# Splitting weights at other times, and a TensorE that works before its tokens come

## The chip, the cores and the metric

The kernel runs on one core of a Trainium2 chip. The metric is the device time of one launch in microseconds (us). Weights, tokens and scratch tensors lie in the chip's memory; all sums are fp32 sums of products of split fp32 numbers, as told below.

## The reference

```python
xn = layernorm(x)                          # x is (8, 1024, 512), no scale or shift
local  = softmax(q @ k.T / sqrt(128)) @ v  # q, k, v = xn @ local_qkv_w, head 128
sparse = the same with sparse_qkv_w, scores below the 102nd largest of their row left out
xp  = xn @ memory_proj_w                   # memory head, 64 memories
mem = concat(xp, softmax(xp @ bank.T) @ bank) @ mem_out_w + mem_out_b
pred = gelu((xn @ pred_in_w + b) @ pred1_w + b) @ pred2_w + b
s = concat(local, sparse, mem, pred) @ warboss_w + warboss_b     # "mixing" weights, 512 x 512
g = silu(relu(xn @ w1 + b1) @ w2 + b2)     # FFN, width 2048 = 16 chunks of 128
out = x + s * g
```

## The kernel before

Every product of two fp32 matrices is made of three products on TensorE (`product`, L70 to L74): each operand is split into a high part (a copy rounded to the type fp32r) and a low part (value minus high part), and high x high, high x low and low x high are summed. A split costs one or two evictions on ScalarE (ACT): the value and its high part; and one subtraction, on VectorE (DVE, helper at L646) or on GpSimd (POOL, helper at L487).

Stage 1 goes through the tokens in 16 halves n = 0 to 15 of 512 tokens. For each half TensorE runs 18 jobs in the order of a list (`JOBS`, and `FIRST_JOBS` for n = 0), each into one of six PSUM banks: mp and pi (12 products of 512 columns each: memory projection, input of the prediction), ql, qs, kl, ks (queries and keys, 12 each), ms (memory scores), p1a, p1b and p2 (prediction), wt (transposed memory weights), tr0 to tr3 (the next half's normalised tokens transposed, 16 transposes of 128x128 in all), mo (memory output), v01 and v23 (values, 24 products of 256 columns each). ScalarE evicts the jobs in the same order. VectorE makes in each half, in this order: the low parts of mp and pi (`act_lo`), the memory softmax, `gelu_hi` and `gelu_lo` (p2 waits for them), the low part of wt (mo waits for it), the low parts of the four transposed token blocks, and then the layer norm of half n+2 (`layer_norm`, L655 to L686). GpSimd makes the low parts of queries, keys, values, mo, p2 and of one FFN chunk per half (`ffn`, behind kl). SyncE issues all DMAs, in one order with its waits: the next tokens, the stored transposed tokens, keys (`store_kv(0)`), the FFN chunk, the tiles of queries and head outputs (`tile_scratch`), the next raw FFN chunk, values.

Half 0 is special. Tokens of half 0 are loaded in four tiles, normalised, and transposed after the whole normalisation (L869), block by block of columns. ScalarE copies each transposed block twice (`tokens`, L519 to L522), a raw copy and the high part, and VectorE subtracts the two. All projection weights are split here, and so are the four 128-row blocks of the mixing weights: ScalarE makes `ww_hi` behind ql (L619), VectorE makes `ww_lo` (`low_mixing`, L720) in two pairs, before `gelu_hi` and before wt's low part. Layer norm 1 is spread over half 0, layer norm 2 over half 1 (`parts`), whose tokens are loaded late (`load_half` behind `store_kv(0)` for n = 1).

In half 14 and 15 the first steps of stage 2 are mixed in: the sparse scores of tile 0 and the search for their 102nd largest value, 13 rounds on VectorE (`first_search`, MAX8 and MATCH_REPLACE8). Two rounds stand in half 15 between the memory maximum and the memory weights (L806 to L809).

Stage 2 has 64 slots of one 128-token tile each; slot m (from 1) has four FFN chunks (f1: 12 products into `hid`, f2: 12 into `acc`), the scores, transposes (L1618) and head outputs. The first FFN weights that stage 2 reads are the ones that stage 1 stored last: `first_ffn` (L414) loads them when the store of the 16th chunk has landed. In slot 1 the order on TensorE is sparse scores, f1 of chunk 0, transposes, f1 of chunk 1, full scores, f2 of chunk 0, f1 of chunk 2, transposes of the full probabilities. VectorE's search in slot 1 takes the row maximum of the full scores in round 2 (L1456) and the reciprocal of their sum in round 3 (L1462).

Of the kernel before, what the change touches and what calls it, by code (L numbers as in the profile page):

```python
# [42 lines left out]
NEWTON = 3  # L43

# [32 lines left out]
def build(nc, x, w, out):  # L77
# [4 lines left out]
    with ExitStack() as outer:  # L82
# [7 lines left out]
        ww_hi, ww_lo = sb("ww_hi", [P, KT, D], F32R), sb("ww_lo", [P, KT, D], F32R)  # L90
# [7 lines left out]
        with nc.sbuf_tensor("ffn", [P, 2, 2, D], F32R) as ffn:  # L98
            pass
        shared = Shared(  # L100
            ident=ident, ww_hi=ww_hi, ww_lo=ww_lo, b2=b2, half_bias=half_bias, small=small, ranks=ranks,
# [49 lines left out]
class Shared:  # L151
# [3 lines left out]
    ww_lo: object  # L155
    b2: object
# [69 lines left out]
def stage1(nc, outer, x, w, xnT_d, kv_d, tile_d, ffn_d, shared):  # L226
# [8 lines left out]
    SM_LOADS, BIAS_LOADS = 4, 5  # L235
    CONSTS = 3

    with ExitStack() as ctx:
# [30 lines left out]
        ww = xnT_raw[:, 1, :, HI, :]  # L269
# [36 lines left out]
        ww_split = sem("ww_split")  # L306
        ln_step = sem("ln_step")
        xn_ready = sem("xn_ready")
        job_done = sem("job_done")
# [29 lines left out]
        def sync(sp):  # L339
# [30 lines left out]
            sp.dma_start(ww[:, :, :], w["warboss_w"].rearrange("(k p) n -> p k n", p=P)).then_inc(ww_in, 16)  # L370
# [46 lines left out]
            def steps(b):  # L417
                for hh in range(2):
# [9 lines left out]
                    if n < LAST - 1 and n != 1:  # L428
                        load_half()
# [17 lines left out]
                    if n == LAST - 1:  # L447
                        first_local()
                    sp.wait_ge(kv_l, 4 * n + 2)
                    store_kv(0)  # L450
                    if n == 1:
                        load_half()

                    sp.wait_ge(ffn_l, n + 1)
                    sp.dma_start(ffn_d[bass.ds(n, 1), :, :, :, :].rearrange("a p i s n -> p (a i s n)"),
                                 ffn[:, :, :, :].bitcast(F32).rearrange("p i s n -> p (i s n)")).then_inc(ffn_st, 16)
# [6 lines left out]

                    sp.wait_ge(ffn_st, 16 * n + 16)
                    if n < LAST:
                        load_ffn(n + 1)
                    else:
                        first_ffn()
# [8 lines left out]
        def gpsimd(pool):  # L477
# [11 lines left out]
            def steps(b):  # L489
                for hh in range(2):  # L490
# [3 lines left out]
                    for name in (name for name in jobs(n) if name in slots):  # L494
# [18 lines left out]
        def scalar(act):  # L513
# [21 lines left out]
            def steps(b):  # L535
                for hh in range(2):
                    n = 2 * b + hh
                    for name in jobs(n):
# [55 lines left out]
                        else:  # L594
# [6 lines left out]
                            if first(n):  # L601
                                act.wait_ge(ww_split, k + 1)
# [41 lines left out]
        def vector(dve):  # L644
# [127 lines left out]
            def steps(b):  # L772
                for hh in range(2):
# [1016 lines left out]
```

## Time and profile before

| | us |
|---|---|
| median of 3 runs | 2559.91 (2559.63 to 2560.24) |
| the profiled execution, its own time | 2559.92 |
| span of its first to last instruction | 2558.1 |
| TensorE busy | 2519.6 (98%) |
| VectorE busy | 2316.3 (91%) |
| ScalarE busy | 1357.9 (53%) |
| GpSimd busy | 1094.0 (43%) |

The span is told in us from its first instruction. In the rows further down PE is TensorE, PEld its weight loads, SPq the DMA queue that SyncE fills. A row of the timeline has start, duration, engine, line, operation, what is written and what is read, and how often; in brackets stands how long the engine was idle before, and for whom. PEclk is the granted clock of TensorE as a share of 2.4 GHz.

### The profile page before, as it was taken

To read this page: it belongs to the slowest core of one execution; us is meant where nothing else is said; L and a number is where in the kernel's file an instruction comes from. 1 tells how busy PE (TensorE), PEld (TensorE's weight loads), DVE (VectorE), ACT (ScalarE), POOL (GpSimd) and SP (SyncE) were. 2 spreads that over 40 slices of the span, in tenths; PEclk is the share of its full clock that TensorE was granted. 3 is DMA by queue.
4 is the path that set the end of the run, shared out by engine and by line. 5 is a ranking of instruction groups with operands and counts; after the bars stand their busy time and mean duration, and the time that the engine had idled before them with its cause. 6 is when DMAs were issued, how large, how long until landed. Compare 5 with 4: busy or idle time off the path is not lost.

```text
span 2558.1 us, 36958 instructions
## 1 busy us (share of the span) xinstructions
PE 2519.6 (98%) x12884; PEld 2144.0 (84%) x12884; DVE 2316.3 (91%) x5184; ACT 1357.9 (53%) x2304; POOL 1094.0 (43%) x847
## 2 busy tenths in 40 slices
PE   7999999999999999999999999999999999999999
PEld 5788888778888888888888888888888888888887
DVE  6666666889999999999999999999999999999996
ACT  5677777744444444444444444444444444444443
POOL 2444554433444444444444444444444444444443
PEclk9999999999999999999999999999999999999999
DMA  7788788874665466556654665466546654665443
GB/s 235 269 306 320 283 308 337 317 271 157 210 219 198 165 209 221 198 165 208 222 198 165 211 218 199 165 212 213 200 165 212 217 197 165 213 215 197 165 157 124
DMA packets 164568, 551.79 MB, mean 216 GB/s; under 512 B 17888, under 2 KB 30880, under 8 KB 156064
## 3 DMA queue, kind: packets, MB, share of 16 engines
q1 hardware_dynamic: 164384, 549.43, 61.2%
q8 instruction: 104, 1.70, 0.3%
q14 instruction: 80, 0.66, 0.1%
HBM read 415.15 MB, written 134.22 MB: 215 GB/s over the span
## 4 chain that ended last, share of the span: by engine, by line
PE 95%; DVE 2%; DMA 1%; ACT 0%; POOL 0%; SPq 0%; issue 0%; ACTq 0%
PE acc L72 9%; PE hid L74 9%; PE hid L72 9%; PE acc L74 9%; PE acc L73 9%; PE hid L73 9%; PE o L74 5%; PE o L73 5%; PE o L72 5%; PE ps L72 5%; PE ps L74 5%; PE ps L73 5%; PE scores L1618 4%; PE scores L74 2%; PE scores L73 2%; PE scores L72 2%
## 5 line engine op out<-in xcount | busy, mean ns | idle before, releaser
L1360 POOL TENSOR_TENSOR h_lo<-h,h_hi 128x512 fp32r<-128x512 f32 x254 | 333.8, 1314 | 811.9 <-ACT h_hi L1257 811.9
L1488 DVE MAX8 ranks<-early 128x8 f32<-128x512 f32 x819 | 564.3, 689 | 13.0
L1508 DVE MATCH_REPLACE8 early<-ranks,early 128x512 f32<-128x512 f32 x756 | 510.8, 676 | 0.0
L1256 ACT ACTIVATE h<-hid,small 128x512 f32<-128x512 f32 x256 | 176.3, 689 | 500.8 <-PE hid L74 500.8
L72 PE MATMUL acc<-w,h_hi 128*128 128x512 f32 x1016 | 408.2, 402 | 0.0
L72 PE MATMUL hid<-xnT,w 128*128 128x512 f32 x1024 | 399.3, 390 | 7.5 <-DMA w<-ffn_scratch 7.5
L74 PE MATMUL hid<-xnT,w 128*128 128x512 f32 x1024 | 399.6, 390 | 0.0
L73 PE MATMUL hid<-xnT,w 128*128 128x512 f32 x1024 | 398.8, 389 | 0.0
L74 PE MATMUL acc<-w,h_lo 128*128 128x512 f32 x1016 | 396.6, 390 | 0.0
L73 PE MATMUL acc<-w,h_hi 128*128 128x512 f32 x1016 | 396.3, 390 | 0.0
L1360 POOL TENSOR_TENSOR pT_s<-pT,pT_s 128x512 fp32r<-128x512 f32 x256 | 326.8, 1299 | 40.9 <-ACT pT_s L1269 40.9
L1492 DVE MAX8 ranks<-early 128x8 f32<-128x512 f32 x441 | 298.0, 676 | 0.0
L1511 DVE MATCH_REPLACE8 early<-ranks,early 128x512 f32<-128x512 f32 x378 | 255.3, 675 | 0.0
L72 PEld LDWEIGHTS hid<-xnT,w 128*128 128x128 f32 x1024 | 192.6, 188 | 48.0 <-DMA w<-ffn_scratch 7.7
L74 PEld LDWEIGHTS hid<-xnT,w 128*128 128x128 f32 x1024 | 192.5, 188 | 40.1
L73 PEld LDWEIGHTS hid<-xnT,w 128*128 128x128 f32 x1024 | 192.6, 188 | 39.9
L74 PEld LDWEIGHTS acc<-w,h_lo 128*128 128x128 f32 x1016 | 190.7, 188 | 41.7
L73 PEld LDWEIGHTS acc<-w,h_hi 128*128 128x128 f32 x1016 | 191.6, 189 | 33.7
L72 PEld LDWEIGHTS acc<-w,h_hi 128*128 128x128 f32 x1016 | 191.2, 188 | 33.6
L487 POOL TENSOR_TENSOR tiles_out<-tiles_out 128x512 fp32r<-128x512 f32 x64 | 104.6, 1635 | 260.4 <-ACT tiles_out L579 235.9
L1257 ACT ACTIVATE h_hi<-hid,small 128x512 fp32r<-128x512 f32 x254 | 173.1, 682 | 0.0
L1269 ACT ACTIVATE pT_s<-scores 128x512 fp32r<-128x512 f32 x256 | 158.1, 618 | 0.0
(224 smaller groups left out, 5496.3 us busy)
## 6 DMA issues: line engine op xcount, KB each, us to landing
w<-ffn_scratch SPq DMA_DIRECT2D x512, 512.0 KB, 4.0
xnT_scratch<-xnT SPq DMA_DIRECT2D x16, 2048.0 KB, 13.5
kv_scratch<-kv_out SPq DMA_DIRECT2D x32, 1024.0 KB, 7.1
tile_scratch<-tiles_out SPq DMA_DIRECT2D x16, 2048.0 KB, 8.7
tl<-tile_scratch SPq DMA_DIRECT2D x64, 512.0 KB, 4.0
xnT<-xnT_scratch SPq DMA_DIRECT2D x60, 512.0 KB, 6.8
ffn_scratch<-ffn SPq DMA_DIRECT2D x16, 1024.0 KB, 6.6
values<-kv_scratch SPq DMA_DIRECT2D x16, 1024.0 KB, 6.5
```

What stands on the lines that cost most here:

```text
L72: nc.tensor.matmul(out, w_hi, x_hi, start=first, stop=False)
L73: nc.tensor.matmul(out, w_hi, x_lo, start=False, stop=False)
L74: return nc.tensor.matmul(out, w_lo, x_hi, start=False, stop=last)
L487: pool.tensor_tensor(value, value.bitcast(F32), hi.bitcast(F32), ALU.subtract).then_inc(ready, 1)
L1256: nc.scalar.activation(h32[:, c % 2, :], hid[:, :], ACT.Relu, bias=bias)
L1257: nc.scalar.activation(h_of(C, c)[0], hid[:, :], ACT.Relu, bias=bias).then_inc(h_h, 1)
L1269: nc.scalar.activation(pT_s[:, j * HTILES:(j + 1) * HTILES, HI, t, :], scores[:, c].rearrange("p (t n) -> p t n", n=P), ACT.Copy)\
L1360: return nc.gpsimd.tensor_tensor(out_, value, hi_.bitcast(F32), ALU.subtract).then_inc(ready, 1)
L1488: l_step = count(nc.vector.max(top_l[:, own], larger[:, :]))
L1492: s_step = count(nc.vector.max(top_s[:, own_s], smaller[:, :]))
L1508: l_step = count(nc.vector.match_replace(larger[:, :], top_l[:, own], larger[:, :], LOWEST))
L1511: s_step = count(nc.vector.match_replace(smaller[:, :], top_s[:, own_s], smaller[:, :], LOWEST))
```

## The change

1. TensorE transposes the identity 72 times into `scores` before tokens come. The first tokens are then transposed tile by tile, each tile as soon as it is normalised (`tile_ready`).
2. `tokens` evicts only the high part; VectorE takes the raw value of the low part from PSUM. The last quarter of the projection weights is split behind the four token blocks.
3. The mixing weights are loaded into the room of `ww_lo` and split one block each in halves 2 to 5: `ww_hi` behind v23's eviction on ScalarE, `ww_lo` behind the layer norm on VectorE. The waits of tr0 to tr3 in half 0 for this split go. The zero rows of `bm_lo` are written at the very start.
4. Layer norm 2 goes to the end of half 0, its tokens are loaded without the special place, and half 1 has no spread parts.
5. The FFN chunk is split behind ks in half 0 and behind qs later (before: behind kl), and GpSimd no longer waits for wt in halves 14 and 15. From half 1 on it is stored before the keys, and the next raw chunk is loaded (in half 15: `first_ffn`) before the tile store is issued.
6. One search round less in half 15 before the memory weights.
7. Stage 2's first two `load_w2` and their wait for the tile stores move behind `load_w1(2)` in slot 1.

```diff
+WARM = 72
-        ww_hi, ww_lo = sb("ww_hi", [P, KT, D], F32R), sb("ww_lo", [P, KT, D], F32R)
+        ww_hi = sb("ww_hi", [P, KT, D], F32R)
+        with nc.sbuf_tensor("ww_raw", [P, KT, D], F32) as ww_raw:
+            pass
+        ww_lo = sb("ww_lo", [P, KT, D], F32R)
...
+    MIXING_AT, MIXING_BEHIND = (2, 3, 4, 5), "v23"
+    FFN_AT = {True: "ks", False: "qs"}
...
-                    if n < LAST - 1 and n != 1:
+                    if n < LAST - 1:
                         load_half()
...
+                    if not first(n):
+                        store_ffn()
                     sp.wait_ge(kv_l, 4 * n + 2)
                     store_kv(0)
-                    if n == 1:
-                        load_half()
-                    (wait for ffn_l, store of the FFN chunk)
+                    if first(n):
+                        store_ffn()
+                    sp.wait_ge(ffn_st, 16 * n + 16)
+                    if n < LAST:
+                        load_ffn(n + 1)
+                    else:
+                        first_ffn()
                     sp.wait_ge(tiles_l, 4 * n + 4)
                     (store of the tiles)
-                    sp.wait_ge(ffn_st, 16 * n + 16)
-                    (load_ffn(n + 1) or first_ffn())
...
-                        if name == "kl":
-                            if n >= LAST - 1:
-                                pool.wait_ge(lo_ready, lo(n, "wt"))
+                        if name == FFN_AT[first(n)]:
                             pool.wait_ge(ffn_h, n + 1)
                             left(ffn[:, :, LOW, :], ffn[:, :, HI, :], ffn_l)
...
             def tokens(k):
                 act.wait_ge(job_done, k + 1)
-                nc.scalar.activation(xnT_raw[:, 0, k, LOW, :], ps[:, k, :], ACT.Copy)
                 nc.scalar.activation(xnT[:, 0, k, HI, :], ps[:, k, :], ACT.Copy).then_inc(bank_read, 1)
...
-            tokens(0)
+            for k in range(KT):
+                tokens(k)
             weights(KT - 1)
-            for k in range(1, KT):
-                tokens(k)
...
-                            if first(n):
-                                act.wait_ge(ww_split, k + 1)
...
-                        if (n, name) == (0, "ql"):
+                        if name == MIXING_BEHIND and n in MIXING_AT:
+                            k = MIXING_AT.index(n)
                             act.wait_ge(ww_in, 16)
-                            for k in range(KT):
-                                nc.scalar.activation(ww_hi[:, k, :], ww[:, k, :], ACT.Copy).then_inc(w_h, 1)
+                            nc.scalar.activation(ww_hi[:, k, :], shared.ww_raw[:, k, :], ACT.Copy).then_inc(ww_h, 1)
...
+            dve.wait_ge(consts, CONSTS)
+            nc.vector.tensor_tensor(bm_lo[MEM:P, :], ident[MEM:P, :], ident[MEM:P, :], ALU.subtract)
             layer_norm(0)
-            parts = {0: layer_norm_parts(1), 1: layer_norm_parts(2)}
+            parts = {0: layer_norm_parts(1)}
...
-                subtract(xnT[:, 0, k, LOW, :], xnT_raw[:, 0, k, LOW, :], xnT[:, 0, k, HI, :])\
+                subtract(xnT[:, 0, k, LOW, :], ps[:, k, :], xnT[:, 0, k, HI, :])\
...
                     if n == LAST:
                         next(rounds)
-                        next(rounds)
...
-                        low_mixing((0, 1))
...
-                    if first(n):
-                        low_mixing((2, 3))
...
-                    if 0 < n < LAST - 1:
+                    if n < LAST - 1:
                         layer_norm(n + 2)
+                    if n in MIXING_AT:
+                        k = MIXING_AT.index(n)
+                        dve.wait_ge(ww_h, k + 1)
+                        subtract(ww_lo[:, k, :], shared.ww_raw[:, k, :], ww_hi[:, k, :])
...
             pe.wait_ge(consts, CONSTS)
-            pe.wait_ge(xn_ready, 1)
-            for k in range(KT):
-                transposes(k, k).then_inc(job_done, 1)
+            for _ in range(WARM):
+                nc.tensor.transpose(scores[:, 0:P], ident[:, :], ident[:, :])
+            for t in range(HTILES):
+                (wait for tile_ready t + 1, for the last tile xn_ready)
+                for k in range(KT):
+                    last = first_transposes(t, k)
+                    if t == HTILES - 1:
+                        last.then_inc(job_done, 1)
...
-            sp.wait_ge(tiles_st, 16 * HALVES)
-            load_w2(1, 1)
-            load_w2(2, 2)
...
                 load_w1(C + 2, c + 2)
+                if m == 1:
+                    sp.wait_ge(tiles_st, 16 * HALVES)
+                    load_w2(1, 1)
+                    load_w2(2, 2)
                 load_w2(C + 3, c + 3)
```

## Rows read from the trace of the kernel before

**Rows 1.** The waits of TensorE, summed: us in total, times, longest.

```profile
PE hid L72 <- DMA w<-ffn_scratch: 7.5, 1, 7.5
PE ps L72 <- DVE gelu_lo L646: 7.0, 2, 5.7
```

**Rows 2.** Windows: span, its length, busy time of PE, PEld, DVE, ACT, POOL, PEclk, DMA.

```profile
46.70:56.00 9.30, 9.30 (x50) 8.20 (x51) 5.14 (x8) 5.88 (x11) 2.58 (x2) 0.78 0.68 282
...
540.00:2558.00 2018.00, 2012.52 (x10086) 1705.10 (x10084) 1947.04 (x4370) 976.16 (x1571) 849.84 (x687) 1.00 0.57 193
```

**Rows 3.** Timeline, the first 20 us.

```profile
12.87 3.65 PE L869 MATMUL ps<-ident,early 128*128 128x128 f32 x16 [12.87 <-DVE early L684]
13.15 0.84 ACT L517 ACTIVATE wp_hi<-tiles_out 128x768 fp32r<-128x768 f32 x1 [0.51 <-DMA tiles_out<-in_L_attn_sparse_qkv_w]
...
13.99 0.60 ACT L521 ACTIVATE xnT_raw<-ps 128x512 f32<-128x512 f32 x1
...
14.49 0.59 ACT L522 ACTIVATE xnT<-ps 128x512 fp32r<-128x512 f32 x1
...
16.70 0.40 PE L73 MATMUL ps<-xnT,wp_hi 128*128 128x512 f32 x1
...
20.15 0.40 PE L74 MATMUL ps<-xnT,wp_lo 128*128 128x512 f32 x1
```

**Rows 4.** Timeline of VectorE, 36 to 48 us.

```profile
38.19 4.44 DVE L646 TENSOR_TENSOR ww_lo<-xnT_raw,ww_hi 128x512 fp32r<-128x512 f32 x2
42.55 1.75 DVE L833 CAST gelu_hi<-gelu 128x1024 fp32r<-128x1024 f32 x1
44.33 2.16 DVE L646 TENSOR_TENSOR gelu_lo<-gelu,gelu_hi 128x1024 fp32r<-128x1024 f32 x1
```

**Rows 5.** Timeline of TensorE: p2 of half 0, mp of halves 1, 2 and 3, ms.

```profile
46.64 0.77 PE L72 MATMUL ps<-gelu_hi,sm_hi 128*128 128x512 f32 x1 [5.68 <-DVE gelu_lo L646]
...
55.37 0.40 PE L72 MATMUL ps<-xnT,wp_hi 128*128 128x512 f32 x1
...
86.31 0.40 PE L72 MATMUL ps<-xnT,wp_hi 128*128 128x512 f32 x1
...
98.17 0.30 PE L924 MATMUL ps<-bkT_s,act_hi 128*128 128x128 f32 x1 [3.51 <-DVE act_lo L646]
...
120.88 0.40 PE L72 MATMUL ps<-xnT,wp_hi 128*128 128x512 f32 x1
```

**Rows 6.** The chain of waits, full halves: start, us, what.

```profile
136.95 0.44 PE ps L938 x4
...
141.52 1.75 PE ps L869 x16
...
166.09 0.44 PE ps L938 x4
```

**Rows 7.** Timeline, layer norm 2 and the tile store of half 1.

```profile
85.89 0.36 SPq L459 DMA_DIRECT2D tile_scratch<-tiles_out  x1
90.20 2.47 DVE L666 BATCH_NORM_STATS2 small<-early 128x6 f32<-128x512 f32 x4 [5.49 <-DMA early<-in_L_attn_x]
97.34 1.28 DVE L646 TENSOR_TENSOR act_lo<-act,act_hi 128x512 fp32r<-128x512 f32 x2
97.72 0.60 ACT L578 ACTIVATE tiles_out<-ps 128x512 f32<-128x512 f32 x1 [4.48 <-DMA tile_scratch<-tiles_out]
```

**Rows 8.** Timeline, from stage 1 to stage 2.

```profile
499.69 0.47 SPq L455 DMA_DIRECT2D ffn_scratch<-ffn  x1
505.89 1.62 SPq L414 DMA_DIRECT2D w<-ffn_scratch  x2
...
513.35 0.68 DVE L1492 MAX8 ranks<-early 128x8 f32<-128x512 f32 x1
...
521.12 1.22 DVE L1456 TENSOR_REDUCE ranks<-scores 128x1 f32<-128x1024 f32 x1 [7.10 <-PE scores L74]
...
526.36 1.09 PE L1618 MATMUL scores<-ident,early 128*128 128x128 f32 x8
```

More of the change, by code:

```diff
@@ L100, in build @@
         shared = Shared(
-            ident=ident, ww_hi=ww_hi, ww_lo=ww_lo, b2=b2, half_bias=half_bias, small=small, ranks=ranks,
+            ident=ident, ww_hi=ww_hi, ww_lo=ww_lo, ww_raw=ww_raw, b2=b2, half_bias=half_bias, small=small, ranks=ranks,
             xnT=xnT, xnT_raw=xnT_raw, ks=ks, kl=kl, tl0=tl0, tl1=tl1, w10=w10,
@@ L155 @@
     ww_lo: object
+    ww_raw: object
     b2: object
@@ L305, in stage1 @@
         w_first = sem("w_first")
-        ww_split = sem("ww_split")
+        ww_h = sem("ww_h")
         ln_step = sem("ln_step")
         xn_ready = sem("xn_ready")
+        tile_ready = sem("tile_ready")
         job_done = sem("job_done")
@@ L448, in steps, with store_ffn @@
                         first_local()
+                    def store_ffn():
+                        sp.wait_ge(ffn_l, n + 1)
+                        sp.dma_start(ffn_d[bass.ds(n, 1), :, :, :, :].rearrange("a p i s n -> p (a i s n)"),
+                                     ffn[:, :, :, :].bitcast(F32).rearrange("p i s n -> p (i s n)")).then_inc(ffn_st, 16)
+                    if not first(n):
+                        store_ffn()
                     sp.wait_ge(kv_l, 4 * n + 2)
                     store_kv(0)
[L451 to L456 removed]
+                    if first(n):
[5 more added lines that the diff above has]
+                        first_ffn()
                     sp.wait_ge(tiles_l, 4 * n + 4)
@@ L462, in steps @@
                         .then_inc(tiles_st, 16)
-                    sp.wait_ge(ffn_st, 16 * n + 16)
[L465 to L468, printed above, removed]
                     sp.wait_ge(kv_l, 4 * n + 4)
@@ L634, in steps @@
                                 .then_inc(shared.pl_ready, 1)
-                        if name == "kl":
+                        if name == FFN_AT[first(n)]:
                             act.wait_ge(ffn_in, 32 * n + 32)
@@ L685, in layer_norm_parts @@
                                                    rstd[:, t:t + 1], ALU.subtract, ALU.mult)
+                    if first(n) and t < HTILES - 1:
+                        last.then_inc(tile_ready, 1)
                 last.then_inc(xn_ready, 1)
@@ L710, in vector @@
             low_weights(QS, 1)
-            def low_mixing(rows):
-                for k in rows:
-                    dve.wait_ge(w_h, 2 + KT + k)
-                    subtract(ww_lo[:, k, :], ww[:, k, :], ww_hi[:, k, :]).then_inc(ww_split, 1)
             def small_weights():
@@ L823, in steps @@
                         dve.wait_ge(bm_out, 1)
-                        subtract(bm_lo[0:MEM, :], bm[0:MEM, :], bm_hi[0:MEM, :])
-                        nc.vector.tensor_tensor(bm_lo[MEM:P, :], bm[MEM:P, :], bm[MEM:P, :], ALU.subtract)\
-                            .then_inc(bm_split, 1)
-                        low_mixing((0, 1))
+                        subtract(bm_lo[0:MEM, :], bm[0:MEM, :], bm_hi[0:MEM, :]).then_inc(bm_split, 1)
                     if n == LAST:
@@ L873, in tensor, with first_transposes @@
             pe.wait_ge(consts, CONSTS)
-            pe.wait_ge(xn_ready, 1)
-            for k in range(KT):
-                transposes(k, k).then_inc(job_done, 1)
+            for _ in range(WARM):
+                nc.tensor.transpose(scores[:, 0:P], ident[:, :], ident[:, :])
+            def first_transposes(t, k):
+                return nc.tensor.transpose(ps[:, k, t * P:(t + 1) * P], xn[:, t, k * P:(k + 1) * P], ident[:, :])
+            for t in range(HTILES):
+                if t < HTILES - 1:
+                    pe.wait_ge(tile_ready, t + 1)
+                else:
+                    pe.wait_ge(xn_ready, 1)
+                for k in range(KT):
+                    last = first_transposes(t, k)
+                    if t == HTILES - 1:
+                        last.then_inc(job_done, 1)
             def bank_projection():
```

3 lines of the change are left out of this document (1 added, 2 removed).

## The prediction

> **What bounds the kernel now.** I read the shares of busy time first: TensorE is busy for 2519.6 of 2558.1 us, so only the 38.5 us in which it idles, and the stretches in which it runs at its lower clock, are to be had without taking work off it. Then TensorE's waits: 7.5 us for a first-layer FFN weight and 7.0 us for `gelu_lo` [rows 1], and 3.5 us for `act_lo` in half 2 [rows 5]; the 12.9 us before the first transpose are the start itself. Then windows around them. After a long wait TensorE also runs slowly: from 46.7 to 56 the granted clock is 0.78 of full, which is 4.1 us at the level of 1.2 GHz instead of 2.4, or 2.0 us lost on top of the wait [rows 2]. From half 3 on the halves follow each other in 29.14 us (136.95 to 166.09) [rows 6] without a wait. In stage 2 TensorE is busy for 2012.5 of 2018 us, and VectorE for 1947.0 of them [rows 2]: both are nearly full there. So what is late on TensorE up to slot 1 moves the end, as long as VectorE comes along.
>
> The sum is made against the profiled execution, 2559.92 us (span 2558.1, 1.8 us around it). It lies 0.01 us from the median of the runs, so both serve.
>
> **Start (edits 1 and 2).** Now the 16 transposes start at 12.87, when all four tiles are normalised, and take 3.65 us, or 0.23 each; in a full half 16 take 1.75 us, or 0.11 each [rows 3, 6]. The durations say that they run at the lower level (the granted clock has no entry for it there). At 16.70 a product takes the 0.40 us that it also takes at 20.15: the level rose within 3.8 us of the first transpose, with little but transposes before it [rows 3]. So the 72 identity transposes from about 1.8 us on should take 3.8 us for 17 at 0.23 and 6.0 us for 55 at 0.11, and be done at 11.6. Tiles come at about 11.3, 11.8, 12.3 and 12.7 and need 0.44 us each: all blocks are transposed at about 13.3, where it was 16.5.
>
> The next limit is ScalarE. It is in the third weight split until 13.99, released by a DMA [rows 3], which the change leaves. Then four high parts, 0.5 us apart as at 13.99 and 14.49 [rows 3], give blocks at 14.6, 15.1, 15.6 and 16.1. VectorE subtracts in 0.64 us each (two take 1.28, [rows 7]): done at 15.2, 15.9, 16.5 and 17.2. Its source in PSUM has no row with this width; between 0.5 and 1.2 us I take 0.64, the row of the same operation and width. The last three products of mp then run from 17.3 to 18.0; now mp ends at 20.15 plus 0.23, 20.4. Gain 2.4. The last weight split follows at 16.1 to 16.9, before VectorE wants it at 17.2. The zeroing of `bm_lo` at the start lies in front of the first tile's arrival: nothing. If TensorE's 2 us of idleness between 13.3 and 15.3 brings the lower level back, 1.5 to 2 us of the gain go.
>
> The Trainium skill speaks against this step: its page "TensorE: Matmul & The Clock Gate", section "Part 4: PE-mode transpose", says that the full clock does not engage for the transpose mode, since it does not count as TensorE being busy. The rise at 16.70 speaks against the rule here. It has a rival of its own below.
>
> **Half 0 (edits 3 and 5).** VectorE's queue is the limit here. The chain from mp's low part to layer norm 1 moves by 2.4 us as a whole. Behind it go two `ww_lo` of 4.44 us and the zero rows; `gelu_hi` 1.75 and `gelu_lo` 2.16 end at 46.5 [rows 4]. Now `gelu_hi` can start at about 34.5 and `gelu_lo` ends at 36.4 to 38.4, by whether GpSimd's work beside it still slows it to these durations. TensorE would be at p2 at 46.64 minus 5.68 minus 2.4, 38.6 [rows 5]: no wait, and no slow stretch. Next comes mo, for wt's low part, about 0.5 us late, since ScalarE's evictions of v01 and wt set it. p2 to v23 takes 7.2 us: mp of half 1 starts at 45.9 instead of 55.37 [rows 5]. Gain to here 9.4 (7.0 of it in this step). Mixing blocks in halves 2 to 5 cost VectorE 0.64 us each before the low part of mp, and ScalarE one 0.6 us copy. That low part is wanted for ms, 8.2 us after mp's start (94.5 against 86.31 [rows 5]); layer norm and low parts take 7.1 and 0.64, and in a full half the norm starts well before mp. They cost nothing; if this cover were gone, 0.64 each, 2.6 together.
>
> **Layer norm 2 and half 1 (edit 4).** In half 0 the norm now stands between tr3 and half 1's first low part. Its length is 97.34 minus 90.20, 7.1 us [rows 7]. FIRST_JOBS puts tr3 last but one, so tr3's low part ends at about 47.2, with `half_bias` 47.6, the norm 54.8, the low part 55.4. ms could start at 45.9 plus 8.2, 54.1: a new wait of 1.4 us. Behind it lies the tile store: load_ffn and the landing of the FFN store go before it, so it is issued at about 48.5. The store of half 1 took from 85.89 to 97.72 until it let ScalarE on [rows 7], so ql's eviction may come at 57 to 60 where it is wanted at 54.4, with the memory softmax behind it on ScalarE from 58: 0 to 2 us more. I take 2.0 for half 1 in all (0.6 to 3.5). Half 1 lasts 30.94 now (86.31 minus 55.37) and 29.14 plus 2.0 then: 0.2 lost.
>
> **Half 2.** It lasts 34.57 now (120.88 minus 86.31) [rows 5], since its tokens come late and the norm ends at 97.3; the wait is 3.51 and the slow stretch behind it costs the rest. With tokens and norm a half earlier it is a full half: 29.14, gain 5.4. Mp of half 3 then starts at 106.3: 14.6 earlier.
>
> **Halves 3 to 13.** Storing the FFN chunk before the keys issues 1 MB some 3 us earlier, and puts 0.5 MB of raw chunk ahead of the tiles. ScalarE's ql eviction is behind the tile store. No wait of TensorE follows by my reckoning: 0 a half, bounded by 0 and 2 (half a load's 4 us).
>
> **Stage 2's entry (edits 5 to 7).** Now the FFN store is issued at 499.69, lands at 505.89, and the load issued then is there at 515.26, 7.5 us after TensorE wanted it [rows 1, 8]. Behind qs instead of behind kl and wt, GpSimd would be done with the chunk at about 494.5; with no key store before it, it is issued 5 us earlier, lands at about 499.5, and the load, now ahead of the 2 MB of tiles, is in by 505: before TensorE wants it. What is late next is VectorE. It is at the end of its second MAX8 of round 2 at 514.03, then idles 7.10 for the full scores, takes the maximum at 521.12, and TensorE transposes the probabilities at 526.36, 5.24 later, without a wait [rows 8]. Without the load's wait the scores are there at 512 to 513, so VectorE goes on at 514.03, and the transposes come at 519.27. Gain 7.1, VectorE's idle time, and not the 7.5 plus a slow stretch that TensorE has. The moved search round changes nothing in VectorE's sum; it lets the memory weights come 2.5 us earlier but leaves VectorE idle for up to 1.6 before `gelu_hi`, against 1 to 1.7 less slowing by GpSimd. Bounds 5.5 and 8.7. `load_w2(1)` now waits for f1 of chunk 0 and the tile store, issued at about 511, wanted at 520: hidden.
>
> **Sum.** 14.6 plus 7.1 is 21.7: 2559.92 minus 21.7 is 2538.2 us.
>
> **Rivals.**
> A, forecast: 2538.2, own range 2533 to 2542; chance 0.72.
> B, the identity transposes leave the clock low. 72 at 0.23 last till 18.4, the 16 real ones 3.7 us more, till 22.1; mp follows at the low level and ends at about 25 to 26.5 instead of 18. That is 7 to 8.5 lost: 2545 to 2547. For it: nothing in the rows, but they show no transposes of a constant alone. The Trainium skill's rule named above would make it so. Chance 0.10.
> C, the end of the wait in half 0 only makes room for the next: GpSimd and ScalarE, which run beside VectorE, hold wt's low part and the tile store of half 0 so that 3 to 5 us of the 14.6 stay: 2541 to 2544. For it: the 4.48 us of ScalarE behind a tile store [rows 7]. Chance 0.12.
> D, the other side: the raw FFN chunk ahead of the tiles delays each tile store so far that ScalarE's ql eviction, and with it the memory softmax, comes too late for wt in every half. Twelve halves lose s each; from 1.8 us a half on the whole gain is gone, and at 2.3 the time is 2566. For it: half 2 already gave ScalarE 4.48 us of waiting there [rows 7]. Against: TensorE didn't wait for it, and the FFN store moves out of the crowd. Chance 0.03.
> E, the change doesn't do what it says at the entry to stage 2: the FFN load is still last there, as DMA queues are full. Then 3 to 7 of the 7.1 stay: 2541 to 2545. Chance 0.03.
>
> **How the numbers follow.** The range 2533 to 2546 holds A, C, E and most of B. About 0.2% (5 us) is what a measurement here tells from no change, so same is 2554.8 to 2565.0: parts of D, and unknown stalls of several kinds together, 0.03. Slower is D's far end, 0.02; faster 0.95.
>
> **What would show it.** In the new trace: identity transposes at 0.23 and then 0.11 us, done near 11.6; mp's last product near 17.8; p2 without a wait near 38.6; mp of half 1 near 45.9, ms of half 1 some 1.4 us late; mp of half 3 near 106.3; halves of 29.14; no wait of `hid` for `w`; instead TensorE idles some 2 us before transposes in slot 1, and VectorE's idle time before L1456 is gone. Wrong would be: halves longer than 29.14, a wait in stage 2 that repeats, transposes at 0.23 to the end.

## Result and profile after

The changed kernel takes 2544.47 us (median of 4 runs, 2543.05 to 2544.64) against 2559.91 us. The ratio on record is 0.9937, 95% interval 0.9925 to 0.9949; the two medians alone give 0.9940, which lies inside. Forecast were 2538.2 us, with 2533 to 2546 as the range. The gain is 15.4 us where 21.7 were forecast. The profiled execution took 2544.64 us, with a span of 2542.8 us against 2558.1.

A cut by halves is the best first look. ScalarE's eviction of mp comes once in each half and has the same place in both kernels. The table gives its start, so the step in the row of half 1 is what half 0 brought, and so on. The rows of slots 1 and 2 are the probability transposes of stage 2 on TensorE; the last row is the end of the span.

| | before | after | gained up to here | gained in this step | forecast |
|---|---|---|---|---|---|
| half 0 | 20.65 | 18.21 | 2.44 | 2.44 | 2.4 |
| half 1 | 58.32 | 52.11 | 6.21 | 3.77 | 7.0 |
| half 2 | 89.26 | 83.20 | 6.06 | -0.15 | -0.2 |
| half 3 | 123.83 | 112.34 | 11.49 | 5.43 | 5.4 |
| half 14 | 444.36 | 433.09 | 11.27 | -0.22 | 0 |
| half 15 | 474.86 | 464.33 | 10.53 | -0.74 | 0 |
| slot 1, transposes | 526.36 | 509.60 | 16.76 | 6.23 | 7.1 |
| slot 2, transposes | 542.44 | 527.31 | 15.13 | -1.63 | 0 |
| end of span | 2558.1 | 2542.8 | 15.3 | 0.2 | 0 |

So three places hold nearly the whole shortfall of 6.4 us: half 0, half 14, and slots 1 and 2.

TensorE's waits after, summed (us in total, times, longest):

```profile
PE scores L1633 <- ACT early L1322: 2.7, 1, 2.7
PE ps L73 <- ACT tiles_out L582: 2.2, 1, 2.2
PE scores L876 <- POOL ident L492: 1.8, 1, 1.8
PE ps L73 <- DVE xnT L650: 1.6, 1, 1.6
...
PE hid L73 <- DMA w<-ffn_scratch: 0.2, 1, 0.2
```

The 7.5 us for `w` and the 7.0 us for `gelu_lo` of [rows 1] are gone (0.2 and none). In their place stand 2.7 us before the transposes of slot 1 and 2.2 us before mo of half 0. Each is followed by a stretch at the lower level of the clock. Windows (stretch, its length, busy time of PE, PEld, DVE, ACT, POOL, then PEclk, DMA share, GB/s):

```profile
43.00:44.00 1.00, 1.00 (x5) 0.77 (x4) 1.00 (x1) 0.13 (x1) 1.00 (x2) 0.58 0.86 360
44.00:46.00 2.00, 2.00 (x11) 1.80 (x9) 1.86 (x2) 1.41 (x3) 1.37 (x2) 0.50 0.96 399
46.00:47.00 1.00, 1.00 (x8) 1.00 (x7) 0.13 (x1) 1.00 (x3) 1.00 (x1) 0.71 1.02 422
...
511.00:513.00 2.00, 2.00 (x6) 1.52 (x6) 2.00 (x5) 1.80 (x4) 2.00 (x2) 0.50 0.98 406
513.00:515.00 2.00, 2.00 (x8) 1.57 (x7) 2.00 (x6) 0.00 (x0) 1.55 (x2) 0.70 1.02 408
...
540.00:2540.00 2000.00, 1997.25 (x10011) 1692.68 (x10009) 1929.24 (x4331) 967.86 (x1556) 842.33 (x681) 1.00 0.57 193
```

A granted clock of 0.50 is 1.2 GHz. Stage 2 is as full as in [rows 2].

The start, in the timeline (start, length, what, idle time before it and what ended it):

```profile
1.77 9.93 PE L876 MATMUL scores<-ident 128*128 128x128 f32 x72 [1.77 <-POOL ident L492]
11.55 1.91 PE L880 MATMUL ps<-ident,early 128*128 128x128 f32 x16
13.64 2.04 ACT L529 ACTIVATE xnT<-ps 128x512 fp32r<-128x512 f32 x4
14.25 2.48 DVE L650 TENSOR_TENSOR xnT<-ps,xnT 128x512 fp32r<-128x512 f32 x4 [0.55 <-ACT xnT L529]
15.09 0.47 PE L73 MATMUL ps<-xnT,wp_hi 128*128 128x512 f32 x1 [1.63 <-DVE xnT L650]
17.72 0.40 PE L75 MATMUL ps<-xnT,wp_lo 128*128 128x512 f32 x1
```

The last product of mp is at 17.72 (forecast 17.8, before 20.15 [rows 3]).

Half 0 and half 1, several engines:

```profile
39.58 2.35 POOL L497 TENSOR_TENSOR ffn<-ffn 128x1024 fp32r<-128x1024 f32 x1
40.06 2.42 DVE L650 TENSOR_TENSOR act_hi<-act,act_hi 64x512 fp32r<-64x512 f32 x1 [2.82 <-ACT act_hi L557]
41.96 0.33 SPq L459 DMA_DIRECT2D ffn_scratch<-ffn  x1
42.51 3.34 DVE L650 TENSOR_TENSOR xnT<-xnT_raw,xnT 128x512 fp32r<-128x512 f32 x2
42.59 0.47 PE L73 MATMUL ps<-act_hi,sm_hi 128*128 128x512 f32 x1 [2.22 <-ACT tiles_out L582]
52.96 0.43 SPq L475 DMA_DIRECT2D tile_scratch<-tiles_out  x1
60.67 0.60 ACT L584 ACTIVATE tiles_out<-ps 128x512 f32<-128x512 f32 x1 [4.57 <-DMA tile_scratch<-tiles_out]
65.98 0.63 PE L952 MATMUL ps<-ident,we 128*128 128x128 f32 x4 [0.75 <-DVE we L821]
```

The wait of mo at 42.59 is put down to ScalarE. But ScalarE's eviction was done at 42.16, and mo needs wt's low part too. That is VectorE's line at 40.06: it takes 2.42 us for 64 partitions, ends at 42.48, and began 0.5 us behind GpSimd's FFN subtraction. p2 came at 38.30, without a wait (46.64 before, [rows 5]).

Half 14 and the entry to stage 2:

```profile
449.17 2.86 POOL L497 TENSOR_TENSOR ffn<-ffn 128x1024 fp32r<-128x1024 f32 x1
454.41 0.47 PE L73 MATMUL ps<-act_hi,sm_hi 128*128 128x512 f32 x1 [0.51 <-DVE act_hi L650]
483.05 0.32 SPq L459 DMA_DIRECT2D ffn_scratch<-ffn  x1
487.53 1.66 SPq L421 DMA_DIRECT2D w<-ffn_scratch  x2
503.88 0.50 PE L73 MATMUL hid<-xnT,w 128*128 128x512 f32 x1 [0.18 <-DMA w<-ffn_scratch]
504.40 1.20 DVE L1471 TENSOR_REDUCE ranks<-scores 128x1 f32<-128x1024 f32 x1
509.60 1.09 PE L1633 MATMUL scores<-ident,early 128*128 128x128 f32 x8 [2.69 <-ACT early L1322]
```

The load of the first FFN weights goes out at 487.53 instead of 505.89 [rows 8]. VectorE reaches its maximum at 504.40 without the 7.10 us of idle time that it had before. TensorE's wait for `w` is 0.18 here, but 0.5 to 1.3 in eight of the traces below (E1, E2, E3, E6, E8 to E11): the load has little room.

### The profile page after: what moved, and what is told of

Its sections match the earlier page's. It is cut to its first block, busy times and chain, and to the rows that moved or that the text cites. A ratio compares the mean times of both kernels' runs of the same rounds, so it can differ in the third digit from the quotient of the medians.

```text
span 2542.8 us, 37090 instructions
## 1 busy us (share of the span) xinstructions
PE 2525.9 (99%) x12956; PEld 2150.9 (85%) x12956; DVE 2325.6 (91%) x5184; ACT 1356.9 (53%) x2300; POOL 1095.4 (43%) x847
## 4 chain that ended last, share of the span: by engine, by line
PE 95%; DVE 2%; ACT 1%; DMA 1%; issue 0%; POOL 0%; SPq 0%; ACTq 0%
PE acc L73 9%; PE acc L75 9%; PE acc L74 9%; PE hid L75 9%; PE hid L74 9%; PE hid L73 9%; PE o L75 5%; PE o L74 5%; PE o L73 5%; PE ps L73 4%; PE ps L75 4%; PE ps L74 4%; PE scores L1633 4%; PE scores L74 2%; PE scores L75 2%; PE scores L73 2%
```

## Experiments

Clock and waits of a kernel are its profiled execution's; where one kernel is set beside another by a few tenths, the table at the end of this section counts from mp's eviction of half 15 to the end, which leaves out how far the start of a run strayed: the first eviction lies between 17.18 and 18.58 in eleven kernels with the same start. Each kernel has one trace, so a half or a slot is told as that execution had it.

One thing strays besides the start, and it is best known before the experiments are read: whether the clock falls behind a wait. Nine kernels have the same code from mp to mo of half 0 and the same wait for mo, 2.22 to 2.26 us. In five (after, E2, E4, E7, E11) the granted clock then fell to 0.50 for some 3.5 us, and half 0 took 33.9; in four (E5, E6, E8, E12) it stayed at 1.00, and half 0 took 32.3. Of E8, whose code is that of after up to stage 2:

```profile
42.97 0.47 PE L73 MATMUL ps<-act_hi,sm_hi 128*128 128x512 f32 x1 [2.23 <-ACT tiles_out L582]
44.00:46.00 2.00, 2.00 (x18) 1.91 (x17) 2.00 (x2) 1.60 (x3) 1.97 (x3) 1.00 0.91 385
```

So 1.6 us of half 0 are a matter of the execution and not of the kernel. At the entry to stage 2 it is the same: eight kernels have the same code from half 15 on, and the clock fell in four of them.

**E1: in half 0 the FFN subtraction waits for wt's low part.**

```diff
                         if name == FFN_AT[first(n)]:
+                            if first(n):
+                                pool.wait_ge(lo_ready, lo(n, "wt"))
```

> The changed kernel (2544.5 us, span 2542.8) with one edit: in half 0 GpSimd waits for wt's low part before it subtracts the FFN chunk. Theory T (GpSimd's subtraction holds VectorE's, and TensorE's wait of 2.22 us for mo then costs the clock as well): wt's low part takes 0.7 us and not 2.42, mo starts at about 41.0 and not 42.59, no slow stretch follows, and mp of half 1 starts 2.5 to 3.2 us earlier than at 49.2. The whole kernel gains at most 0.5, since ScalarE's ql eviction in half 1 still waits for a tile store that is not issued before 52.96, so that TensorE's wait before wt in half 1 grows from 0.75 to 3 us or more. Rival R (ScalarE's order of evictions holds mo): mo stays within 0.3 us of 42.59, total within 0.3.

Measured: 2544.02 us (3 runs). The low part fell to 0.7 us, mo came at 40.10 with a wait of 0.48, the clock held, and half 0 fell from 33.90 to 31.69. Half 1 grew from 31.09 to 33.69. The cause of the mo wait is shown, and the fix gains nothing: GpSimd's subtractions now run beside four subtractions of `xnT` on VectorE, which take 7.83 us, the norm behind them is late, and ms waits 2.83 us for `act_lo`. I had expected the new wait before wt, for the tile store; there it is 0.24.

**E2: in half 0 the tile store is issued before the wait for the FFN store.** The wait and the load become `next_ffn()`, called right behind the tile store when `first(n)`.

```diff
-                    sp.wait_ge(ffn_st, 16 * n + 16)
-                    if n < LAST:
-                        load_ffn(n + 1)
...
+                    if not first(n):
+                        next_ffn()
                     sp.wait_ge(tiles_l, 4 * n + 4)
...
+                    if first(n):
+                        next_ffn()
```

> The changed kernel with one edit: in half 0 SyncE issues the tile store before it waits for the FFN store, as before the change. Theory T: the tile store goes out at 47.3 and not at 52.96, ql's eviction in half 1 comes without a wait at 56.1 and not 60.67, the wait of 0.75 us before wt in half 1 goes, and perhaps the 0.66 before mo: 0.8 to 1.4 us in all, about 2543.3. Rival: the DMA queues are the limit and the store lands at 59 or later in any case: gain under 0.3.

Measured: 2540.43 us (2 runs). The store goes out at 46.33 instead of 52.96, ScalarE doesn't wait for it, and half 1 takes 29.13, a full half's time: 2.0 us gained there. That is what the edit brings; expected were 0.8 to 1.4. The profiled execution is 4.6 us shorter than that of after: another 1.0 of it is the start's scatter, and 1.6 the slow stretch of slot 1, which didn't come in this execution.

**E3: both.**

> Both edits together. Theory T: neither is worth its sum alone; together 3.5 to 4.5 us, 2540 to 2541, with mp of half 1 at 46 to 46.7 and mp of half 2 some 3.5 to 4 us earlier than at 80.3. Rival R (evictions hold mo): what e2 gains alone, about 1 us.

Measured: 2546.28 us (3 runs), where 2540 to 2541 was expected. Half 0 took 31.66, half 1 35.28. The timeline of half 0:

```profile
40.70 2.39 POOL L502 TENSOR_TENSOR ffn<-ffn 128x1024 fp32r<-128x1024 f32 x1 [1.17 <-DVE act_hi L657]
40.72 0.47 PE L73 MATMUL ps<-act_hi,sm_hi 128*128 128x512 f32 x1 [0.48 <-issue]
40.90 7.82 DVE L657 TENSOR_TENSOR xnT<-xnT_raw,xnT 128x512 fp32r<-128x512 f32 x4 [0.29 <-ACT xnT L615]
...
44.74 3.44 POOL L502 TENSOR_TENSOR tiles_out<-tiles_out 128x512 fp32r<-128x512 f32 x2
50.07 2.46 DVE L677 BATCH_NORM_STATS2 small<-early 128x6 f32<-128x512 f32 x4
```

Four subtractions, 0.69 us each without a neighbour, take 7.82 us while GpSimd subtracts without a pause. Layer norm 2 starts at 50.07, ms waits 2.86 us for it, and from 58 to 64 the granted clock is 0.50.

**E4: in half 14 the FFN subtraction goes back behind kl and wt's low part.** ScalarE's high part of the chunk goes behind kl with it.

```diff
+    def ffn_at(n):
+        return "kl" if n == LAST - 1 else FFN_AT[n == 0]
...
-                        if name == FFN_AT[first(n)]:
+                        if name == ffn_at(n):
+                            if ffn_at(n) == "kl":
+                                pool.wait_ge(lo_ready, lo(n, "wt"))
```

> The changed kernel with the FFN chunk of half 14 alone back behind kl and behind wt's low part on GpSimd. Theory T (in half 14 the FFN subtraction at 449.2 stretches VectorE's first search steps, 1.78 to 2.89 us, and wt's low part, 0.69 to 1.65, so that mo waits 0.51 us): the half takes 30.5 us as before the change and not 31.24, total 0.7 us less, 2543.7. Rival: the 0.74 us come from the moved DMAs, and stay.

Measured: 2543.12 us (3 runs). Half 14 takes 30.48 instead of 31.24 (30.5 before the change), so its loss is this subtraction's place. The transposes of slot 1 come at 509.81 all the same, after a wait of 2.76: the 0.76 us are gone again by then. Mo of half 15 waits 1.25 us instead of 0.33, and VectorE sets the entry. Its four subtractions of `xnT` in half 14 take 5.68 us now instead of 2.49.

**E5 and E6: no identity transposes, and 24 of them.** `WARM = 72` becomes 0 and 24.

> The changed kernel without the 72 identity transposes (WARM = 0); all else stays. Theory T (identity transposes bring the full clock, and transposes count): the 16 real transposes start at 11.4 and not behind the identities, at 0.21 each, end at about 14.8 instead of 13.4; the level rises some 3.8 us after 11.4, before mp's first product, so that mp ends 0.7 to 1.3 us later than at 18.0: 2545.2 to 2545.8. Rival (the page's rule that a transpose does not count, or a clock that the idle time before mp takes back anyway): the level rises only some 3.5 us after mp's first product, mp ends 2 us and more later, 2546.5 or more.

> 24 identity transposes and not 72. They end at 6 to 6.6 us, and TensorE idles for 5 us before the first tile. Theory T (the level is kept by steady work until just before the tokens; an idle time as long as 3.5 us lost it in half 2 of the kernel before): the real transposes run at the lower level again, as without identities, 0.7 to 1.3 us worse than 72. Rival (a rise once reached lasts over 5 us of idle time): real transposes at 0.11 us, time as with 72.

Measured: 2544.58 and 2545.23 us (3 runs each). TensorE without them:

```profile
11.25 3.65 PE L880 MATMUL ps<-ident,early 128*128 128x128 f32 x16 [11.25 <-DVE early L688]
15.77 0.47 PE L73 MATMUL ps<-xnT,wp_hi 128*128 128x512 f32 x1 [0.86 <-DVE xnT L650]
```

and with 24:

```profile
1.78 4.62 PE L876 MATMUL scores<-ident 128*128 128x128 f32 x24 [1.78 <-POOL ident L492]
10.79 3.68 PE L880 MATMUL ps<-ident,early 128*128 128x128 f32 x16 [4.39 <-DVE early L688]
15.33 0.76 PE L73 MATMUL ps<-xnT,wp_hi 128*128 128x512 f32 x1 [0.86 <-DVE xnT L650]
15.89 0.63 PE L74 MATMUL ps<-xnT,wp_hi 128*128 128x512 f32 x1
```

```profile
6.00:11.00 5.00, 0.61 (x5) 0.37 (x4) 4.08 (x20) 1.90 (x2) 0.00 (x0) 0.79 1.14 303
11.00:17.00 6.00, 5.14 (x20) 4.48 (x20) 4.75 (x9) 4.48 (x7) 0.00 (x0) 0.50 0.84 154
```

Without them the 16 real transposes run at 0.23 us each, and the products are at full clock from 15.77, as in the kernel before [rows 3]. ScalarE's copies come 0.7 us later (14.30 against 13.64), since they wait for TensorE, and mp's eviction comes at 18.87 against 18.21. So 72 transposes of the identity are worth about 0.7 us at mp, the least that was expected, and nothing at the end that these runs can tell. By subtraction, most of the 2.44 us at the start come from the transposes tile by tile, with the lows from the accumulators; no run undoes those two.

The 24 take 4.62 us, which is 17 at 0.23 and 7 at 0.11: they raise the level. Then TensorE idles 4.39 us and the level falls. I had expected that much, and then a start as without any. But the same 16 real transposes that precede full clock in E5 do not here: eight products of mp run at 0.63 to 0.76 us, and its eviction comes at 20.18. With one execution of each, and a clock that differs between executions of the same code, it isn't shown that 24 are worse than none in general.

**E7: in half 15 the FFN subtraction, its store and the first load go back to their old places.** E4's edit with `n == LAST`, and on SP's queue:

```diff
-                    if not first(n):
+                    if not first(n) and n < LAST:
                         store_ffn()
                     sp.wait_ge(kv_l, 4 * n + 2)
                     store_kv(0)
-                    if first(n):
+                    if first(n) or n == LAST:
                         store_ffn()
...
+                    if n == LAST:
+                        sp.wait_ge(ffn_st, 16 * n + 16)
+                        first_ffn()
```

> The changed kernel with half 15's FFN chunk, its store and the load after it in the old places (GpSimd behind kl and wt, store behind the keys, load behind the tile store). Stage 2's order stays changed. Theory T: the wait of 7.5 us for the FFN weight in slot 1 is back with its slow stretch, and VectorE's idle time of 7 us before the maximum; the transposes of slot 1 come 51 to 52 us after mp's eviction in half 15 and not 45.3, the total is 4 to 5.5 us above the changed kernel, 2548.5 to 2550. Rival: stage 2's moved load_w2 did the work: the wait stays near 0.2.

Measured: 2547.87 us (4 runs), 0.6 below what was expected. The wait for `w` is back (7.3 us), VectorE idles before its maximum:

```profile
509.43 1.23 DVE L1478 TENSOR_REDUCE ranks<-scores 128x1 f32<-128x1024 f32 x1 [6.27 <-PE scores L75]
```

and the transposes of slot 1 come 49.81 us after mp's eviction instead of 45.27; expected were 51 to 52.

**E8: in slot 1 the maximum is taken a round earlier.**

```diff
                 r_max, r_inverse = R_MAX[T % HTILES], R_INVERSE[T % HTILES]
+                if m == 1:
+                    r_max, r_inverse = 1, 2
```

> The changed kernel with one edit: in slot 1 alone VectorE takes the row maximum of the full scores in round 1 of its search and the reciprocal in round 2, one round (2.5 us) earlier. Theory T (VectorE's order is the limit at the entry to stage 2, and TensorE's wait of 2.7 us there costs the clock too): the wait before the transposes of slot 1 falls to 0 to 0.4, no slow stretch follows, slot 1 to slot 2 takes 16.1 to 16.3 and not 17.7: 3.5 to 4.3 us less, 2540.5 to 2541. Rival (DMAs or ScalarE hold the entry): less than 1 us.

Measured: 2544.15 us (3 runs), where 2540.5 to 2541 was expected. TensorE no longer waits for the probabilities in slot 1 (1.02 us for `w` stay), the clock holds there, and slot 2's transposes come 60.05 us after the eviction instead of 62.98. Then, in the list of TensorE's work from 560 to 600:

```profile
574.59 1.09 PE L1635 MATMUL scores<-ident,early 128*128 128x128 f32 x8 [2.08 <-ACT early L1322]
```

VectorE is busy for 39.5 of those 40 us. What TensorE had gained it waits for some slots later: from the entry to about 575 us VectorE leaves no room, whatever the order inside a slot. From mp's eviction of half 15 to the end the edit brings nothing: 2077.9 us in E8 and 2076.9 in E10, against 2077.0 where the clock held without it.

**E9: as E2, with GpSimd's FFN subtraction of half 0 behind its v23 subtraction. E10: E9 and E8 in one kernel.**

```diff
+    FFN_LOW_AT = {True: "v23", False: "qs"}
...
+                    if first(n):
+                        store_ffn()
+                        next_ffn()
...
-                        if name == FFN_AT[first(n)]:
+                        if name == FFN_LOW_AT[first(n)]:
```

The second addition stands behind the second key store; what half 0 issued ahead of the tile store is gone.

> As e2 (half 0: tile and kv stores issued before the wait for the FFN store), and besides GpSimd's FFN subtraction of half 0 goes behind its v23 subtraction, so that it no longer runs beside VectorE's low part of wt. Theory P (two separate stalls of half 0 and half 1, and e3 fell only because the subtraction stood beside VectorE's four xnT subtractions): wt low part about 0.7 us, the product mo starts near 40.5, half 0 takes 31.0 to 32.3 us between the mp evictions (after: 33.9), half 1 takes 29.1 to 29.5 (31.1), median 2537.5 to 2540. Rival Q (VectorE's whole load in half 0 is the limit and the gain only moves): half 0 about 31.7, but half 1 31 or more because LN(2) and ms come late as in e1 and e3, median 2542 or more. A third outcome: the FFN rows of the next half are now stored and loaded later and TensorE waits for w in half 1.

> e9 and e8 in one kernel. If the entry to stage 2 is VectorE's alone (its idle gone in e8 and the 2.9 us gained at slot 2 given back by a 2.1 us wait in slot 4 for ScalarE's early copy behind VectorE), the two add to no more than e9 alone: median within 1 us of e9, and a wait of 1 to 3 us before prob transposes by 600 us. Rival: max in round 1 is worth its 2 to 3 us once the halves ahead of it are shorter: median 2 or more below e9.

Measured: for E9 2541.50 us (2541.06 to 2541.89, 5 runs; ratio 0.9927, 0.9914 to 0.9939), between its two theories, and for E10 2540.92 us (2540.05 to 2544.41, 5 runs; 0.9927, 0.9915 to 0.9940). E9, half 0 and half 1:

```profile
39.63 1.39 DVE L657 TENSOR_TENSOR act_hi<-act,act_hi 64x512 fp32r<-64x512 f32 x1 [2.80 <-ACT act_hi L564]
41.05 0.69 DVE L657 TENSOR_TENSOR xnT<-xnT_raw,xnT 128x512 fp32r<-128x512 f32 x1
41.12 0.47 PE L73 MATMUL ps<-act_hi,sm_hi 128*128 128x512 f32 x1 [1.18 <-ACT xnT L615]
48.71 2.40 POOL L504 TENSOR_TENSOR ffn<-ffn 128x1024 fp32r<-128x1024 f32 x1
49.70 1.43 DVE L683 TENSOR_SCALAR small<-small 128x4 f32<-128x4 f32 x1
55.18 1.29 DVE L657 TENSOR_TENSOR act_lo<-act,act_hi 128x512 fp32r<-128x512 f32 x2
56.01 0.30 PE L945 MATMUL ps<-bkT_s,act_hi 128*128 128x128 f32 x1 [1.57 <-DVE act_lo L657]
```

Half 0 takes 31.24: mp's eviction of half 1 is at 49.04, where the forecast's 45.9 for mp's first product corresponds to 48.9 (the two are 2.95 apart); 0.4 us of that agreement is an early start, as the first eviction is at 17.80. And the new wait that was forecast for ms, 1.4 us, is there with 1.57, but the size is luck. The norm starts at 46.79, 0.8 earlier than forecast, and one of its small steps (49.70, 0.17 us in after) takes 1.43 beside GpSimd's FFN subtraction at its new place: without that encounter some 0.3 us of the wait would be left, an estimate from these rows. Behind it the clock fell in E9 (0.50 from 58 to 60) and not in E10, with the same 1.57 and the same code: half 1 takes 32.55 in one and 30.93 in the other. So neither theory stands whole: in half 0 mo's wait is 1.18 instead of 2.22, and the stall of half 1 changes from the tile store to layer norm 2. E10 adds nothing that the runs can tell from E9, as expected of a VectorE-bound entry; the wait by 600 us, expected at 1 to 3, shrank to 0.64. Both beat the changed kernel by 3 to 4 us: every run of E9 is below every one of its runs, all but one of E10's, and both of E2's. The ratios' intervals overlap, since they carry the scatter of the kernel before.

**E11: layer norm 2 and its load go back to their old places.**

```diff
-                    if n < LAST - 1:
+                    if n < LAST - 1 and n != 1:
                         load_half()
...
+                    if n == 1:
+                        load_half()
...
-            parts = {0: layer_norm_parts(1)}
+            parts = {0: layer_norm_parts(1), 1: layer_norm_parts(2)}
...
-                    if n < LAST - 1:
+                    if 0 < n < LAST - 1:
                         layer_norm(n + 2)
```

> One part undone: the token load and LN(2) of half 1 go back to their old places (LN(2) in two parts inside half 1, the load after the mixing store). If this part is worth what half 2 shows (before 34.57, after 29.14): half 2 about 34.5, others as after, median 2549 to 2550 (5 above after). Rival: the 1.4 us of half 1 (31.09 against 29.14) is LN(2)'s, so half 1 falls to about 29.5 and the loss is only 3.5 to 4: median near 2548.

Measured: 2548.27 us (4 runs). Half 2 takes 34.49 again (wait for `act_lo` 3.55), as expected. But half 1 took 32.30 and not the 31.09 of after or less: with VectorE's norm inside it, `we` waits 1.44 and p2 1.29 us. The median lies near the 2548 of the rival by luck, as its mechanism (a shorter half 1) did not come: the start was 0.7 early and the clock held in slot 1.

**E12: both search rounds of half 15 in a row behind ms, as before.**

```diff
                     if n == LAST:
+                        next(rounds)
                         next(rounds)
```

> One part undone: in half 15 the first slot's softmax round beside the low part of wt goes back to its old place, two rounds in a row behind ms. If VectorE is busy without a gap there, only the order changes: median within 1 us of after. Rival: the gelu split and wt wait behind the round, TensorE waits in half 15 for them and the entry is later: half 15 to slot 1 longer than 45.3 by 1 to 2 us, median 2545.5 to 2546.5.

Measured: 2546.89 us (4 runs): my expectation fell, the rival holds and was priced too low. TensorE waits 5.06 us for the memory weights in half 15. They stand behind the two rounds on VectorE, but the second round is only 2.5 us:

```profile
477.89 4.98 DVE L818 TENSOR_SCALAR we<-we,small 128x64 f32<-128x64 f32 x4
479.26 2.34 POOL L497 TENSOR_TENSOR ffn<-ffn 128x1024 fp32r<-128x1024 f32 x1
483.35 1.09 PE L953 MATMUL ps<-ident,we 128*128 128x128 f32 x4 [5.06 <-DVE we L822]
```

The scaling of `we`, 0.74 us in after (at 475.91), takes 4.98 here: a round later it meets GpSimd, which subtracts from 478.03 to 482.82 without a pause. In the kernel before the two rounds stood there too and the scaling took 0.74, at 488.95: as late behind mp's eviction as here, but ahead of GpSimd's next subtraction, which began at 489.98. So 4.2 us are lost in the encounter with GpSimd; the round's own time only changes its place.

VectorE itself then idles only 1.02 us before slot 1, yet the slot's transposes come 48.92 us after mp's eviction instead of 45.27.

From mp's eviction of half 15 on, in us:

| | to slot 1 | to slot 2 | to the end |
|---|---|---|---|
| before | 51.50 | 67.58 | 2083.2 |
| after, E1, E3, E5 (clock falls) | 45.27 | 62.98 | 2078.5 |
| E2, E6, E9, E11 (clock holds) | 45.27 | 61.38 | 2077.0 |
| E7 FFN chunk old | 49.81 | 65.93 | 2081.6 |
| E8 maximum early | 43.26 | 60.05 | 2077.9 |
| E10 maximum early | 43.10 | 60.42 | 2076.9 |
| E12 round old | 48.92 | 65.02 | 2080.6 |

## Why the prediction was right, and where it was short

The time fell into the range, but not into A's own 2533 to 2542. What came is the forecast's gains together with rival C, which had a chance of 0.12: 3.1 of the 14.6 us up to half 3 stayed, behind wt's low part and the tile store of half 0, as C has it. The range held it since it was drawn over C as well; of B it held less than "most", as B is 2545 to 2547 and the range ends at 2546. The wait that each edit was to remove went as forecast. Half 0 and the entry to stage 2 were mis-sized, and half 14 was not in the sum. Shown by an edit that undoes them are the parts of half 2 and of the entry; that the moved mixing weights (edit 3) ended the wait for `gelu_lo` in half 0 is read from the trace alone, where that wait is gone.

*Start, 2.4 us: 2.44.* The second digit is luck: the eleven kernels with this start lie 2.1 to 3.5 us below the one trace of before. The identities took 9.93 us (forecast 3.8 plus 6.0), which is the count of transposes at either level: 17 at 0.23 and 55 at 0.11. Rival B fell by these rows: transposes of a constant alone raised the level, and E6 shows it again with 24. Against the rule of the Trainium skill named in the prediction ("TensorE: Matmul & The Clock Gate", "Part 4: PE-mode transpose"), transposes count here. The two idle microseconds that I feared (1.63) cost no level. But E5 says that the gain isn't the identities': they bring about 0.7 us to mp.

*Half 0, 7.0 us: 3.77.* This is the step that failed in size. "About 0.5 us late, since ScalarE's evictions of v01 and wt set it" was the sentence: mo was 2.22 us late, and another 1.6 us went at the lower clock. It is rival C. I had counted VectorE's low part of wt as 0.69, and GpSimd's FFN subtraction beside it as nothing, although [rows 4] show VectorE's subtraction stretched in just this way. E1 takes the overlap away and gets 2.2 of it, E9 gets 2.66; in both the clock held, and against the kernels of the same half 0 in which it held as well (32.3) they get 0.6 and 1.1. The 1.6 us are a matter of the execution, as nine kernels with one and the same code and wait showed. What decides isn't shown. Nor would they have shortened the kernel by as much: where the clock held (E5, E6, E8, E12) half 1 grew from 31.09 to 31.91 to 33.01, and the two halves together took 64.2 to 65.4 against 64.99 in after.

*Half 1, -0.2: -0.15, for another reason, so by luck.* The layer norm's wait of 1.4 didn't come, as mp was 3.2 later than forecast. The tile store did, and later than forecast: issued at 52.96 and not at 48.5, behind the landing of an FFN store that had gone out at 41.96, it held ScalarE's eviction for 4.57 us and TensorE for 0.75 and 0.66 further on. E2 shows the store's part (2.0), E9 the norm's when half 0 is nearly as short as forecast (1.57, of which 1.3 is GpSimd's new place).

*Half 2, 5.4: 5.43.* E11 gives the same from the other side: 34.49 against 29.14.

*Halves 3 to 13, 0: -0.22.* Halves 3 to 6, each with a mixing block split at its beginning, took 29.17 to 29.21 instead of 29.14; all others 29.14. Rival D fell: nothing repeats.

*Half 14, 0: -0.74.* Not forecast: GpSimd's FFN subtraction behind qs runs beside the search and the low part of wt on VectorE (E4). In E4's trace undoing it brought nothing by slot 1, as the entry is VectorE's.

*Entry, 7.1: 6.23, then -1.63.* The mechanism is as forecast: no wait for `w` (0.18), VectorE's 7.10 us of idleness gone, TensorE waiting instead, 2.69 before slot 1's transposes where some 2 were forecast. The step that failed is that this wait was priced at nothing: in after, E1, E3, E4 and E5 the clock fell behind waits of 1.9 to 2.8 us (to 0.50 between 510 and 515) and cost 1.6; in E2, E6, E9 and E11 it held after waits of 1.6 to 2.4 us. "The moved search round changes nothing in VectorE's sum" holds for the rounds alone; the round's place decides what meets GpSimd, and leaving it would have cost 3.6 us (E12). The FFN chunk's way is worth 4.5 (E7). The kernel before, with both undone, stands 6.2 behind and not 8.2: there the memory weights did not meet GpSimd (0.74 us for the scaling). No run undoes both.

Of the 6.4 us short, 3.2 are half 0, 0.7 half 14, 0.9 the entry and 1.6 the clock behind it.

## What to carry to other kernels

When a wait of several microseconds is removed, look at what the other engines do at the new moment: here the instruction next in line met a GpSimd subtraction that had been out of its way. Price each wait of TensorE with the slow stretch that may follow it, 1.6 us here, as a part of the range and not as a certainty, and don't explain a difference of that size between two kernels from one trace of each. Near a stage that another engine bounds, gains on TensorE alone (half 14, slot 1) are given back within a few tens of microseconds; count the bounding engine's idle time and take no more than that.

## What the runs showed of the hardware

VectorE and GpSimd slow each other when both subtract from SBUF. VectorE's 64x512 subtraction takes 0.7 us alone (E3) and 2.42 beside GpSimd's FFN subtraction (2.35 us) in after; four of 128x512 take 7.82 us beside a busy GpSimd (E3), and one takes 0.69 without it (E9). GpSimd's own 128x512 takes 1.7 us there and 1.3 alone. VectorE's scaling of four 128x64 blocks took 4.98 us beside GpSimd (E12) and 0.74 alone. The low part at 40.06 ends at 42.48, 0.55 behind the end of GpSimd's instruction at 41.93, as if it had waited for that and then run. The Trainium skill says as much ("SBUF — State Buffer", "SBUF: two separate sides"): a VectorE operation with two inputs in SBUF and a GpSimd one take turns on a shared pair of ports, for a whole instruction each; the trace agrees. The start's subtractions, with one source in PSUM and GpSimd idle, took 0.62 us each (2.48 for four).

A burst of transposes alone raises the level, and idleness takes it back: 72 went from 0.23 to 0.11 us each; behind 24 and 4.39 us of idleness mp ran at 1.2 GHz, where it ran at 2.4 in the traces with 72 (after) and with none (E5).

The same wait can cost two prices. 2.22 to 2.26 us before mo were followed by some 3.5 us at 1.2 GHz in five of nine executions, for 1.6 us, and by none in four; so were 1.57 us before ms in E9, and not in E10.
